# Moving one DMA group in SyncE's order: the key read goes behind the query write

## The reference

```python
x = x + L0_xattn(layernorm(x), ctx, ctx, ...)      # correlation over time lags, one mix for all batches
x = x + L0_ffn(layernorm(x), ...)                  # 8 experts, top 1
x = x + L1_xattn(layernorm(x), ctx, ctx, mask, ...)
x = x + L1_ffn(layernorm(x), w_gate, w_up, w_down) # quantized gate/up/down, inner size 1024
```

```python
q = split_heads(query @ Wq.T + bq); k = split_heads(key @ Wk.T + bk); v = split_heads(value @ Wv.T + bv)
scores = einsum('bhqd,bhkd->bhqk', q, k) / sqrt(16)
scores = where(mask == 0, -1e9, scores)
p = softmax(scores, axis=-1)
x = einsum('bhqk,bhkd->bhqd', p, v)
```

## Time and profile before

| | |
|---|---|
| time, median of 3 runs | 1837.02 us (1830.69 to 1839.14) |
| profiled execution | 1837.02 us, span 1835.1 us |
| busy: PE, PEld | 1579.6 us (86%), 1163.8 us (63%) |
| busy: DVE, ACT, POOL | 1209.4 us (66%), 1095.1 us (60%), 771.2 us (42%) |
| DMA moved | 147.25 MB, mean 80 GB/s |

### The profile page before, as it was taken

How to read it: one execution, slowest core, us unless ns; L and a number is a source line. 1 busy time by engine, 2 the same in 40 slices (tenths; PEclk the granted TensorE clock), 3 DMA queues, 4 the chain that set the end, 5 groups by cost and what they waited for, 6 DMA issues and landing times.

```text
span 1835.1 us, 34724 instructions
## 1 busy us (share of the span) xinstructions
PE 1579.6 (86%) x10422; PEld 1163.8 (63%) x10422; DVE 1209.4 (66%) x3300; ACT 1095.1 (60%) x2418; POOL 771.2 (42%) x962
## 2 busy tenths in 40 slices
PE   5941789999999989998999899989999899999764
PEld 4821566766666666676766666767766666777542
DVE  5874355777767767776766677767777677777633
ACT  1210235766666667665666666667776566666663
POOL 2345333444444444443444444444444444444221
PEclk9975789999999999999999999999999999999886
DMA  8711333233333323232333333333223123332200
GB/s 269 224 49 46 87 77 77 77 83 83 83 73 82 83 63 73 73 76 60 83 83 83 84 83 83 83 73 83 72 76 83 45 70 82 83 83 66 54 13 12
DMA packets 148988, 147.25 MB, mean 80 GB/s; under 512 B 10930, under 2 KB 147772, under 8 KB 148540
## 3 DMA queue, kind: packets, MB, share of 16 engines
q1 hardware_dynamic: 148796, 144.92, 30.4%
HBM read 99.79 MB, written 42.99 MB: 78 GB/s over the span
## 4 chain that ended last, share of the span: by engine, by line
PE 39%; issue 19%; DVE 17%; DMA 10%; POOL 8%; ACT 5%; SPq 2%; DVEq 0%; POOLq 0%; ACTq 0%
PE bank L1381 14%; PE bank L1302 6%; DMA qs<-qsplit_d 5%; PE bank L1275 4%; DMA qsplit_d<-pl 4%; PE bank L1249 3%; DVE hm L1084 3%; PE bank L1264 3%; POOL hid L640 2%; DVE mx L1036 2%; DVE bn L854 2%; PE bank L1228 1%; POOL rs L613 1%; POOL pl L661 1%; DVE mv L858 1%
## 5 line engine op out<-in xcount | busy, mean ns | idle before, releaser
L786 ACT ACTIVATE pt<-bank 128x512 f32<-128x512 f32 x512 | 302.4, 591 | 212.7 <-PE bank L1249 212.5
L1036 DVE TENSOR_REDUCE mx<-bank 128x2 f32<-128x512 f32 x512 | 333.6, 683 | 55.9 <-PE bank L1302 55.4
L635 POOL TENSOR_TENSOR x<-x,et 128x256 f32<-128x256 f32 x256 | 190.2, 743 | 289.9 <-ACT et L820 289.8
L640 POOL TENSOR_TENSOR hid<-hid,t 128x256 f32<-128x256 f32 x256 | 187.6, 733 | 164.4 <-DVE t L1078 161.1
L1302 PE MATMUL bank<-ks,qs 96*128 96x256 f32 x1024 | 226.0, 304 | 34.7 <-DMA qs<-qsplit_d 17.4
L1249 PE MATMUL bank<-qs,ks 98*128 98x256 f32 x1024 | 233.2, 310 | 13.1 <-ACT pt L786 9.0
L1302 PEld LDWEIGHTS bank<-ks,qs 96*128 96x128 f32 x1024 | 167.5, 192 | 110.8 <-issue 40.3
L1249 PEld LDWEIGHTS bank<-qs,ks 98*128 98x128 f32 x1024 | 159.0, 193 | 53.6 <-ACT pt L786 25.9
L1381 PE MATMUL bank<-ewh,xah 128*128 128x512 f32 x512 | 178.7, 431 | 11.2 <-issue 11.2
L854 DVE BATCH_NORM_STATS2 bn<-x 128x6 f32<-128x256 f32 x256 | 95.8, 416 | 121.6 <-POOL x L644 89.0
L1078 DVE SCALAR_TENSOR_TENSOR t<-th,bank 128x256 f32<-128x256 f32 x256 | 107.0, 418 | 98.9 <-ACT th L832 90.4
(11 more groups left out here) (184 smaller groups left out, 3189.9 us busy)
## 6 DMA issues: line engine op xcount, KB each, us to landing
ks<-ksplit_d SPq DMA_DIRECT2D x96, 256.0 KB
qs<-qsplit_d SPq DMA_DIRECT2D x96, 256.0 KB, 4.5
x<-in_x SPq DMA_DIRECT2D x32, 256.0 KB, 3.6
va<-in_ctxT SPq DMA_DIRECT2D x32, 256.0 KB, 3.5
xl<-in_x SPq DMA_DIRECT2D x32, 256.0 KB
ct<-in_ctxT SPq DMA_DIRECT2D x32, 256.0 KB, 5.0
ksplit_d<-ph SPq DMA_DIRECT2D x32, 256.0 KB, 2.2
ksplit_d<-pl SPq DMA_DIRECT2D x32, 256.0 KB, 2.5
```

Of the source, the lines that this page charges most:

```text
L635: pool.tensor_tensor(x3[:, b.quad, t], x3[:, b.quad, t], et[:], ALU.add).then_inc(e_sum[t], 1)
L640: pool.tensor_tensor(part_, part_, t1[:], ALU.mult).then_inc(hid_made[c % 2], 1)
L786: act.activation(pt[:, s % 4].rearrange("p a c -> p (a c)"), cbank[:, :], ACT.Exp).then_inc(ex_made[s % 4], 1)
L1036: dve.tensor_reduce(mx[:, t, 2 * p:2 * p + 2], shared[:].rearrange("p (h s) -> p h s", h=2), AX_X, ALU.max).then_inc(mx_made[t], 1)
```

## The change

The shift of `k_read` on SyncE goes from -94 to -38 ticks. Its place in a step goes from age 2, tick 90 (440 - 94 = 346) to age 3, tick 18 (440 - 38 = 402): the next step, between `q_write` (tick 12) and `q_read` (tick 47) of the same batch. No other job changes its place, and the instructions are the same.

```diff
 LATER = {
     "sp": {
-        "k_write": -21, "store": 210, "k_read": -94, "load": 107, "q_read": -18, "q_write": 30,
+        "k_write": -21, "store": 210, "k_read": -38, "load": 107, "q_read": -18, "q_write": 30,
         "max_row": -175,
     },
```

## The result

The changed kernel takes 1914.1 us (median of 4 runs, 1909.9 to 1918.1) beside 1838.1 us of the kernel before on the same chip: a ratio of 1.042, 95% interval 1.039 to 1.045, 76 us more. That is the forecast direction and twice the forecast size (37.5 us), outside the range.

What follows compares the result with a forecast made beforehand. In 18 of 32 steps the period was taken to run POOL's `pl`, query write, query read, TensorE's L1302. Delays of 10 x 1.4 + 8 x 1.7 + 9 x 1.1 = 37.5 us on 1837.0 gave 1874.5; range 1848 to 1900.

Steps and rivals of the forecast that it cites:

- Whether a later start of L1302 is a longer step ... I count it in full: TensorE, 93% busy over two steps, can hardly make up a later L1302, so the whole delay counts: 37.5 us.
- What moves earlier, at nothing: On SyncE the loads come 2.9 us earlier; counted as nothing, since the mask load still waits for VectorE's L965.
- What SyncE adds: The key read's 2.9 us on SyncE mostly fill the wait for the query write; query read issued about 0.5 us later.
- What the DMA engines add: Key read takes 3.7 us of engine time against about 2 us idle; L1302 starts 1.4 us later in such steps.
- the higher of the two bounds: Steps with a late query write: L1302 starts 0.1 or, with backlog on one engine, 2.0 us later; 1.7 taken for 8.
- The 5 steps with the issue gap pay nothing: In five steps TensorE's issue gap at L1381 covers the later query read; without the gap, 1.4 us each, 7 us.
- VectorE's cover: VectorE's L969 waits for later key DMAs but finishes 0.4 us before L854's wait for POOL ends; priced at nothing.
- rival 3: Keys land over 0.4 us later than forecast, so VectorE's L969 delays L854 and reduction L1036; 1902 us, chance 0.15.
- It fits: Rival: key read needs only about 2.5 us, issue delay falls into slack; 1837 to 1842 us, no difference, chance 0.11.
- Faster: Rival: eight late query-write landings are backlog from the key read's burst; moving it gains 9 us, 1828, chance 0.05.

Runs made afterwards that it cites:

- the run with five small reads: Kernel before, keys read in their old place, plus five extra 16 KB key reads where the change puts the key read; 1853.4 us, ratio 1.009.
- keys last: Kernel before with all of k_read moved one place further than in the change, behind the query read; 2008.2 us, ratio 1.094.

## Why the prediction was wrong, step by step

The step that failed is *"Whether a later start of L1302 is a longer step ... I count it in full"*. The wait came near the forecast, 42.2 us where the sum had 37.5, but a later start of L1302 cost more than in full: TensorE's busy time over the same matmuls grew by 30.3 us, which the sum had at nothing. By groups of steps, in us, from the two profiled executions:

| steps | forecast | longer by | of it L1302's wait | of it TensorE's busy time |
|---|---|---|---|---|
| ahead of the first query write | 0 | 3.2 | 0 | 3.8 |
| first four | 5.3 | 15.9 | 11.2 | 4.6 |
| ordinary, 8 with a late query write before | 13.6 | 7.8 | 4.2 | 3.4 |
| ordinary, the other 14 | 17.2 | 34.6 | 23.7 | 10.6 |
| 5 at the loop boundary | 0 | 10.8 | 0 | 4.7 |
| from the last query write on | 1.4 | 6.2 | 3.0 | 3.3 |

That the waits sum to nearly the forecast is in part luck: the late-landing steps were priced three times too high, and the other ordinary steps and the first four too low.

- *What moves earlier, at nothing*: nothing speaks against it. The loads came earlier, and no run shows a gain from it.
- *What SyncE adds*: about right. The query read is issued 0.5 to 0.6 us later in steps without a backlog (4.0 against 3.4 us after the write), and the run with five small reads prices a shift of 1.0 us at 17 us.
- *What the DMA engines add*: the mechanism was right, as the full windows, the runs with one and two reads and the run with five small ones show; the sizes were not. In the late-landing steps the higher of the two bounds was too high: L1302 started about 12 us after the write in them as in the others, 0.5 us later than before and not 1.7. In the steps without a wait it was too low: L1302 started 1.9 us later and not 1.1, since the sum put it at 11.1 us after the query write and it came at 11.6 to 12.5. In the first four steps of the pipeline the sum was too low: TensorE reaches L1302 early there and waited 4.3, 4.7, 3.0 and 1.6 us, and from the first query write to the fifth it took 191.8 instead of 175.9 us.
- *"The 5 steps with the issue gap pay nothing"*: wrong. From query write to query write these five grew by 1.0 to 4.5 us, 10.8 in all. ScalarE's `otn` waits there with no releaser in the profile, at the loop boundary, 15.9 us instead of 9.3. It is long where key or other data are in the queues just then (two reads moved: 15.6; both store moved and write cut: 14.2) and short where they aren't (keys last: 8.9; small reads: 9.6; one read moved: 10.0). That the fetch of instructions queues behind the data is a guess; no run isolates it.
- *"... I count it in full"*: the step that failed. After idle waits of 1.6 to 2.7 us TensorE's granted clock was 0.50 for a while in 11 of the 22 ordinary steps, and its work in them became 14 us longer. These 14 us vanished when TensorE was kept busy in the wait. The other 16 us of busy time lie outside the ordinary steps, and their cause is in part open. Forecast 37.5 for the wait, measured 42.2 + 30.3 + 6.6.
- *VectorE's cover*: the 0.4 us were not there (26 waits, 85.4 us), as rival 3 had it, but its price was nought: freed, the time stayed.
- *"It fits"* is refuted for three reads and true for one. *"Faster"* rested on a backlog ahead of the query write. That backlog exists: with the store moved no query write lands late, and nothing measurable is gained (8 us at most). The keys may have a part in it, for with one or two of their reads moved and the store in its place only 2 and 3 ordinary steps had a late landing instead of 8; no run isolates that.

## What to carry to other kernels

A DMA that nobody waits for is not free where it stands directly ahead of one that somebody does: price it by its engine time beyond the idle gap, and look for the gap in the DMA share by windows. The Trainium skill's advice to issue early and wait late (DMA: Bandwidth & Descriptors, Rules for kernel authors) held here for the keys at 9 us ahead of the query write, where no engine waited for them. When a stall on TensorE grows from a few tenths of a microsecond to some two microseconds, ask also for its clock: compare its busy time over the same instructions, before and after. And the longest new wait in a list (85 us on VectorE) can be worth nothing, while a 12 us gain came from writing the high part before GpSimd's low part is ready.

## What the runs showed of the hardware that was not expected

- The granted clock of TensorE fell to 0.50 after waits of 1.6 to 2.7 us in 11 of 22 ordinary steps, and stayed at 1.00 in the 11 others, whose waits were 1.3 to 2.2 us. The waits of the kernel before, under 1.3 us in ordinary steps but for one of 1.7, did it in none. A pair of L1381 took 1.05 us instead of 0.63, and TensorE's busy time in ordinary steps was 1002.7 instead of 988.7 us.
- 1.7 us of otherwise useless matmuls in each of 26 waits made the program 14 us shorter, give or take 8.
